# Graph attention over an 8192 x 8192 adjacency: last steps of the row maxima on GpSimd, a sixth PSUM bank in layer 1, x rows on chip, levels by quarters

## The reference

```python
e = leaky_relu(u[:, None] + v[None, :], 0.2)      # 8192 x 8192
e = where(adj > 0, e, -9e15)
att = softmax(e, axis=1)                           # needs the row maximum
h = elu(att @ features)                            # features: 8192 x 64
# layer 0:   x = layernorm(x + elu(att @ ent + x))
# layer 1,2: h = 0.2 * x + 0.8 * elu(att @ (h W)); a small MLP over all h, layernorm
```

## Time and profile before

| what | value |
|---|---|
| median of 3 runs | 3390.24 us (3382.48 to 3395.13) |
| profiled execution | 3391.65 us, its span 3389.8 us |
| mean granted TensorE clock | 0.986 |
| PE / DVE / ACT / POOL busy in the span | 90% / 84% / 67% / 8% |
| DMA moved | 679.11 MB |

### The profile page before, as it was taken

How to read it: one execution, slowest core, us unless ns; L and a number is a source line. 1 busy time by engine, 2 the same in 40 slices (tenths; PEclk the granted TensorE clock), 3 DMA queues, 4 the chain that set the end, 5 groups by cost and what they waited for, 6 DMA issues and landing times. The chain is left out here.

```text
span 3389.8 us, 53702 instructions
## 1 busy us (share of the span) xinstructions
PE 3053.4 (90%) x20369; PEld 1080.6 (32%) x20447; DVE 2862.4 (84%) x5292; ACT 2282.4 (67%) x3934; POOL 287.8 (8%) x330
## 2 busy tenths in 40 slices
PE   1599999999999998799999999997999999999998
PEld 0133333333333333233333333332333333333333
DVE  5688888888888875899999999987888888888886
ACT  0367777777777676577877777774666666666665
POOL 0000000000000000000000000001122112212211
PEclk9999999999999999899999999998999999999999
DMA  9999999999999951312121212216577767766764
GB/s 308 359 347 343 343 343 344 336 346 346 343 343 348 331 157 54 114 64 109 66 106 72 104 75 103 75 63 173 149 163 177 173 158 164 194 161 161 174 142 81
DMA packets 441749, 679.11 MB, mean 200 GB/s; under 512 B 297474, under 2 KB 318082, under 8 KB 416914
## 3 DMA queue, kind: packets, MB, share of 16 engines
q1 hardware_dynamic: 409458, 564.40, 51.3%
q0 software_dynamic: 32032, 111.27, 16.4%
HBM read 430.10 MB, written 77.69 MB: 150 GB/s over the span
## 5 line engine op out<-in xcount | busy, mean ns | idle before, releaser
L1242 DVE SCALAR_TENSOR_TENSOR eps<-ua,v8col,cb 128x512 f32<-128x512 f32 x2800 | 1960.5, 753 | 243.4 <-ACT prob L640 180.1
L640 ACT ACTIVATE prob<-eps,v2col 128x512 f32<-128x512 f32 x2564 | 1641.2, 688 | 635.6 <-PE eps L813 622.6
L854 PE MATMUL acc<-prob,feat 128*64 128x512 f32 x5128 | 1333.7, 599 | 6.3 <-ACT acc_s L645 6.3
L813 PE MATMUL eps<-nt,nbig 128*64 128x512 fp8e4 (+1 forms) x5444 | 1022.5, 386 | 150.6 <-DVE eps L1242 142.8
L813 PEld LDWEIGHTS eps<-nt,nbig 128*64 128x64 bf16 (+1 forms) x5444 | 327.4, 109 | 1115.0 <-DVE eps L1242 726.5
L1051 DVE TENSOR_SCALAR mi<-stage 128x1024 uint8<-128x1024 int32 x512 | 353.5, 692 | 132.7 <-DMA stage<-in_adj_dram 131.5
L854 PEld LDWEIGHTS acc<-prob,feat 128*64 128x64 f32 x5128 | 338.1, 136 | 256.0 <-issue 94.2
L640 ACT ACTIVATE stage<-eps,v2col 128x512 f32<-128x512 f32 x336 | 214.3, 686 | 95.6 <-PE eps L813 93.9
L863 PE MATMUL den<-prob,ones 128*32 128x512 f32 x2048 | 246.4, 599 | 0.0
L1081 DVE TENSOR_SCALAR edges<-nt 128x2048 int32<-128x2048 int32 x192 | 234.1, 1219 | 7.1 <-PE misc L824 7.0
L824 PE MATMUL misc<-edges,oneh 128*32 128x512 fp8e4 x3072 | 190.9, 391 | 52.7 <-DVE edges L1081 37.9
(11 more groups left out here) (174 smaller groups left out, 1686.8 us busy)
## 6 DMA issues: line engine op xcount, KB each, us to landing
stage<-in_adj_dram SPq DMA_DIRECT2D x512, 512.0 KB, 6.4
nt<-nt_d SPq DMA_DIRECT2D x128, 1024.0 KB, 6.1
nt_d<-nt SPq DMA_DIRECT2D x64, 1024.0 KB, 7.1
prob<-prob POOLq DMA_DIRECT2D x96, 512.0 KB, 5.8
stage<-stage POOLq DMA_DIRECT2D x64, 512.0 KB, 6.4
mi<-mi POOLq DMA_DIRECT2D x32, 512.0 KB, 6.5
ub<-u_d SPq DMA_DIRECT2D x48, 256.0 KB, 5.3
xy_d<-xin POOLq DMA_DIRECT2D x32, 256.0 KB, 3.2
```

Source lines behind the costliest of these rows:

```text
L640: nc.scalar.activation(weights(l, b, j), eps[:, j % ES, :], ACT.Exp, bias=v2col[:, j:j + 1]).then_inc(s_p, 1)
L813: mm = nc.tensor.matmul(et[c:c + cols, :], nbig[:, c:c + cols], edge, start=False, stop=True, skip_group_check=True, tile_position=(0, c))
L854: mm = nc.tensor.matmul(acc[h:h + C, :], feat[:, l % 2, j, 0:C], weights(l, b, j), start=(k == 0), stop=(k == NT // 2 - 1))
L1242: dv.scalar_tensor_tensor(eps[:, j % ES, :], ua[:, par, :], v8col[:, j:j + 1], cb[:, par, :], ALU.add, ALU.max).then_inc(s_fill, 1)
```

## The change

1. **GpSimd makes the maxima.** For blocks 1 to 15 of each layer DVE stops at `kmax` (4 operations, now `highest_levels`). The rest is a new `row_maxima` on POOL: one operation ahead of the wait, then 13 in a chain with ten waits on its own results. Block 0 of each layer stays on DVE.
2. **A sixth bank in layer 1.** The idle `den` bank joins the five.
3. **x rows on chip.** Layer 0 reads x from `feat`, where it lies already, and the 16 loads into `xin` go.
4. **Levels by quarters.** `oneh` is made in four parts with a semaphore each, so that PE counts quarter m as soon as it is there. All four edge quarters of the next layer's block 0 are made during the last block before (two were made at the layer's start), two of them in the staging buffer of layer 0.
5. **Steps of edges and counts.** `T_XOR` and `T_HIST` are spread: counts at t = 33, 36, 40, 43 where they stood in pairs at 35 and 43.

The core of the diff:

```diff
+P_STEPS = 10
+HEAD_AT = 5
+BANKS = (ES, ES + 1, ES)
-T_XOR = (29, 32, 40, 41)
-T_HIST = (35, 35, 43, 43)
+T_XOR = (29, 32, 39, 42)
+T_HIST = (33, 36, 40, 43)
...
+        def edge_place(l, b, m):
+            if l > 0 and b == 0 and m >= 2:
+                return spare[:, m - 2, :]
+            return edges[:, m % 2, :]
...
+        def bank(l, j):
+
+            n = j % BANKS[l]
+            return den[:, :] if n == ES else eps[:, n, :]
+
         def freed(l, b, j):
 
-            if j >= ES:
-                return tile(l, b, j) - ES + 1
-            last = max(i for i in range(NT) if i % ES == j)
+            if j >= BANKS[l]:
+                return tile(l, b, j) - BANKS[l] + 1
+            k = l if b else l - 1
+            last = max(i for i in range(NT) if i % BANKS[k] == j % BANKS[k])
             return tile(l, b, last) - NT + 1
...
+            def row_maxima(l, b, par):
+
+                at = P_STEPS * (later(l, b) - 1)
+                u = vucol[:, l % 2, 1, bass.ds(b * RT, RT)]
+                gp = nc.gpsimd
+
+                def step(ins, n):
+                    ins.then_inc(s_pseq, 1)
+                    pool.wait_ge(s_pseq, at + n)
+
+                gp.tensor_scalar(up[:, :], u, ALPHA, None, ALU.mult)
+                pool.wait_ge(s_kmax, later(l, b))
+                gp.tensor_scalar(emp[:, par, :], kmax[:, :], 0.5, None, ALU.is_le)
+                step(gp.tensor_scalar(vm[:, :], kmax[:, :], gst[:, 5:6], gst[:, 7:8], ALU.mult, ALU.add), 1)
+                step(gp.tensor_scalar(vm[:, :], vm[:, :], gst[:, 6:7], None, ALU.max), 2)
+                step(gp.tensor_tensor(ns[:, :], vm[:, :], u, ALU.add), 3)
+                gp.tensor_scalar(r1[:, :], ns[:, :], 0.0, 1.0 - ALPHA, ALU.max, ALU.mult)
+                step(gp.tensor_scalar(nm[:, :], ns[:, :], ALPHA, None, ALU.mult), 4)
+                step(gp.tensor_tensor(nm[:, :], nm[:, :], r1[:, :], ALU.add), 5)
+                step(gp.tensor_tensor(nm[:, :], up[:, :], nm[:, :], ALU.subtract), 6)
+                pool.wait_ge(s_mt, blk(l, b))
+                step(gp.tensor_copy(parts[:, :, 0], nm[:, :]), 7)
+                step(gp.tensor_tensor(r1[:, :], nm[:, :], parts[:, :, 0], ALU.subtract), 8)
+                step(gp.tensor_copy(parts[:, :, 1], r1[:, :]), 9)
+                step(gp.tensor_tensor(nm[:, :], r1[:, :], parts[:, :, 1], ALU.subtract), 10)
+                gp.tensor_copy(parts[:, :, 2], nm[:, :]).then_inc(s_split, 1)
...
             for l in range(2):
                 for b in range(NB):
-                    tail(l, b)
+                    if b > 0:
+                        tail(l, b - 1)
+                    if b < NB - 1:
+                        row_maxima(l, b + 1, 1 - b % 2)
+                tail(l, NB - 1)
             for b in range(NB):
                 for g in range(NT // DEN):
+                    if g == HEAD_AT and b < NB - 1:
+                        row_maxima(2, b + 1, 1 - b % 2)
...
-                pe.wait_ge(s_oneh, l + 1)
                 for m in range(MV):
+                    pe.wait_ge(s_oneh, l * MV + m + 1)
                     count_edges(l, 0, m)
...
-                step(dv.tensor_tensor(oneh[:, :, :], over(kk[:, :], "p (t o) -> p t o"),
-                                      over(iota[:, :], "p (o k) -> p o k"), ALU.is_equal), s_startseq, at + 11)
-                step(dv.tensor_tensor(oneh[:, :, :], oneh[:, :, :], over(ww[:, :].bitcast(F32), "p (t o) -> p t o"),
-                                      ALU.mult), s_startseq, at + 12)
+                for m in range(MV):
+                    q = slice(m * MT, (m + 1) * MT)
+                    dv.tensor_tensor(oneh[:, q, :], over(kk[:, q], "p (t o) -> p t o"),
+                                     over(iota[:, :], "p (o k) -> p o k"), ALU.is_equal).then_inc(s_startseq, 1)
+                    dve.wait_ge(s_startseq, at + 11 + m)
+                    dv.tensor_tensor(oneh[:, q, :], oneh[:, q, :], over(ww[:, q].bitcast(F32), "p (t o) -> p t o"),
+                                     ALU.mult).then_inc(s_oneh, 1)
```

More of the change, by code:

```diff
@@ L301, in blk, with later @@
             return l * NB + b
+        def later(l, b):
+            return l * (NB - 1) + b
         def tile(l, b, j):
@@ L423, in xin_load @@
             def xin_load(l, b):
[L424 to L427, removed]
+                sp.dma_start(xin[:, :, :], xy_v[l - 1, b]).then_inc(s_xin, 16)
             def xin_free(l, b):
-                if b == 0 and l != 1:
+                if b == 0 and l == 2:
                     return
@@ L488, in body @@
                 def body(b, par, head, tail):
-                    if tail:
+                    if tail and l > 0:
                         xin_free(l, b - 1)
@@ L639, in probs @@
                 act.wait_ge(s_z, tile(l, b, j) + 1)
-                nc.scalar.activation(weights(l, b, j), eps[:, j % ES, :], ACT.Exp,
+                nc.scalar.activation(weights(l, b, j), bank(l, j), ACT.Exp,
                                      bias=v2col[:, j:j + 1]).then_inc(s_p, 1)
@@ L803, in mask_scores @@
                 on_act = j in ON_ACT[l]
-                et = eps[:, j % ES, :]
+                et = bank(l, j)
                 m, o = divmod(j, MT)
@@ L824, in count_edges @@
                         mm = nc.tensor.matmul(misc[s * HB:(s + 1) * HB, :], oneh[:, m * MT + j, :],
-                                              half_block(edges[:, n % 2, :], m, j), start=(m == 0 and k == 0),
+                                              half_block(edge_place(l, b, m), m, j), start=(m == 0 and k == 0),
                                               stop=(m == MV - 1 and k == MT // 4 - 1), skip_group_check=True,
@@ L1113, in row_maxima, with highest_levels @@
                      s_headseq, at + 8)
+            def highest_levels(l, b):
+                n = later(l, b) - 1
+                dve.wait_ge(s_fold, blk(l, b) + 1)
+                dve.wait_ge(s_split, blk(l, b))
+                counts = misc[:, 0:RT * HB].bitcast(I32).rearrange("p (r k) -> p r k", k=HB)
+                base = kstep[:, :].rearrange("p (o k) -> p o k", o=1).broadcast_to([P, RT, HB])
+                step(dv.tensor_scalar(he[:, :, :], counts, 23, None, ALU.logical_shift_right), s_kseq, 3 * n + 1)
+                step(dv.scalar_tensor_tensor(hx[:, :, :], he[:, :, :], 0, base, ALU.is_gt, ALU.mult), s_kseq, 3 * n + 2)
+                step(dv.tensor_tensor(hx[:, :, :], hx[:, :, :], he[:, :, :], ALU.add), s_kseq, 3 * n + 3)
+                dv.tensor_reduce(kmax[:, :], hx[:, :, :], AX, ALU.max).then_inc(s_kmax, 1)
             def split_first(l, b, at):
@@ L1156, in tail_elu @@
                 step(dv.tensor_tensor(z[:, :, :], g[:, :, 0:C], spread(rden[:, :]), ALU.mult), seq, at + 3)
-                dve.wait_ge(s_xin, 16 * (blk(l, b) + 1))
                 if l == 0:
-                    step(dv.tensor_tensor(z[:, :, :], z[:, :, :], xin[:, :, 0:C], ALU.add), seq, at + 4)
+                    step(dv.tensor_tensor(z[:, :, :], z[:, :, :], x_rows(b), ALU.add), seq, at + 4)
+                else:
+                    dve.wait_ge(s_xin, 16 * (blk(l, b) - NB + 1))
                 if not (l == 0 and b == 0):
@@ L1343, in _ @@
                     dve.wait_ge(s_oe, 4 * blk(l, 0))
+                    if l == 1:
+                        dv.memset(feat[:, 1, :, C - 1:C], 1.0).then_inc(s_one, 1)
                     bounds(l)
                     levels(l)
-                    for m in range(2, MV):
-                        make_edges(l, 0, m)
                     for part in range(3):
@@ L1365, in body @@
                         if not head_ and l < NLAYER - 1:
-                            for m in range(2):
-                                if t == T_XOR[m + 2]:
+                            for m in range(MV):
+                                if t == T_XOR[m]:
                                     make_edges(l + 1, 0, m)
```

50 lines of the change are left out of this document (35 added, 15 removed).

## The result

| | before | after |
|---|---|---|
| median of 4 runs each, same chip, us | 3389.47 | 3453.02 |
| ratio, 95% interval | | 1.0191, 1.0175 to 1.0208 |
| profiled execution: time, span, us | 3391.65, 3389.8 | 3455.08, 3453.3 |
| mean granted clock | 0.986 | 0.973 |

The change made the kernel slower by 63.6 us. 3370 was predicted, in a range that ends at 3415.

What follows compares the result with a forecast made beforehand. PE was taken to bound layers 0 and 2, PE and DVE level in layer 1. Layer 2 -9, layer 1 -3, layer 0 -1 and between layers -7 us: -20 from 3390.24 gave 3370 us, range 3352 to 3390, span 3305 to 3415.

Steps and rivals of the forecast that it cites:

- which mechanism: POOL's chain after `kmax`: each step waits for the end of a running fill, one per 0.66 us, without holding DVE.
- The rival of a step that is too long for a period: POOL's chain: a step over 0.6 us costs two fills; 3540 us, or 3410 to 3450 if slightly longer; chance 0.16.
- eleven steps; two of them hold two operations that can go through one opening: POOL's chain after `kmax`: 13 operations with ten waits make eleven steps, turn at +7.1 us in layer 1, +6.7 in layer 2.
- The second rival: POOL's chain: each of 13 operations takes its own opening, or DVE is held; gains gone, 3392 us; chance 0.20.
- in the place of waits of about 2 us that go: PE's turn: POOL late by 2.8 us in layer 1 and 1.4 in layer 2, replacing PE's waits for fills.
- a PE that comes 0.8 later, with a sixth bank filled ahead of it, does not wait so: Layer 1 tail: PE's 0.97 us wait for DVE goes, as PE turns 0.8 us later with more filled ahead.
- the forecast's -0.2: Layer 1: turn 0.8 us later, set against the tail wait that goes; -0.2 us a block, -3 us in all.
- the boundaries: Between layers: counting starts 3.7 us sooner with `oneh` in quarters, counts unbroken; twice, -7 us.
- Layer 0: Layer 0: turn unchanged at +6.8 us, 0; the x rows save 16 loads on full DMA engines, -1 us.
- group 5's DMAs: POOL's queue in layer 2: two DMAs behind the chain land at +13.4, taken at +15.5, 2 us to spare: 0.

Runs made afterwards that it cites:

- the filler: Kernel before with only the maxima on GpSimd, plus 14 unused matmuls by PE while it waits at layer 1's turn: 3441.49 us, ratio 1.0160.
- the three kernels compared: Changed kernel (3453.02 us), kernel before with only GpSimd maxima (3460.28 us), and the latter plus 14 unused matmuls in layer 1 (3441.49 us); layer 2 blocks compared by low clock.
- GpSimd alone: Kernel before with only the maxima moved to GpSimd, five banks and the old steps, loads and levels: 3460.28 us, ratio 1.0200.
- The later turn: Changed kernel with the turn at t = 60 instead of 56 and the spread at 61 instead of 57: 3467.46 us, ratio 1.0221.

## Why the prediction was wrong

Of the 84 us between the forecast of -20 and the +63.5 of span, 43 lie in layer 1 and 39 in layer 2.

- **Right: which mechanism.** POOL is paced by the fills, 0.66 us apart; the fills aren't held; ten of them end at +6.6 in layer 1; PE arrives at +4.3; a free step takes 0.27 us (0.25 was taken). The rival of a step that is too long for a period is out: an operation takes 0.20 us alone.
- **Wrong: "eleven steps; two of them hold two operations that can go through one opening".** None of them does: `emp` and `vm`, and likewise `r1` (`r` in the rows) and `nm`, each take an opening of their own. And a scalar read by a pointer takes one more, three of them in the chain. So 16 openings stand where eleven steps were counted. The turn is at +8.35 and +8.00, not at +7.1 and +6.7: 1.25 and 1.3 us too early in the forecast, some 38 us over 30 blocks. The second rival had the first half of this (13 openings, 3392 us); no rival had the pointers.
- **Wrong: a wait of PE was priced by its length.** The forecast put a POOL that is late by 2.8 and 1.4 us "in the place of waits of about 2 us that go", and counted both by their length. The short waits that went (1.4 us in the block of the earlier trace rows) had left the granted clock at 1.00; the one long wait in their place comes with 3.4 us at 0.50. That was in no term: 1.25 us a block in layer 1 by the filler, 1.3 to 2.0 in layer 2 by the blocks compared, 38 to 49 us over 30 blocks.
- **Wrong: "a PE that comes 0.8 later, with a sixth bank filled ahead of it, does not wait so".** The wait in the tail is 0.97 us before and after, with the turn 2.1 us later. So the 0.97 us a block that this was to give back didn't come; the rest of the change gives 0.37. Turn 1.25, clock 1.25 and this 0.97, less 0.37, are the 3.1 us a block between the forecast's -0.2 and the measured +2.89.
- These close the blocks. Layer 1: +2.08 by the turn, +1.25 by the clock, -0.37 by the rest of the change (56.48 against 56.85 us) make +2.96; measured +2.89. That a later turn is a longer block, us for us, was counted on in the forecast and holds both ways: with the head at tile 52 in four parts the turn of layer 1 is 1.14 us sooner than with the old head on DVE and the block 1.15 shorter (1.13 and 1.11 in layer 2). Layer 2: in the three kernels compared, blocks without the stretch of low clock last 66.6 to 66.9 us, 0.5 to 0.8 above before, where the turn is 0.4 to 0.7 later; with it 68.2 to 68.7, and after, where every block has it, 68.21.
- **Right for what the quarters do, not for the sum: the boundaries.** 3.7 us twice were forecast; after, the first is 3.6 shorter and the second 1.2 longer. With the maxima on DVE both are shorter, by 3.5 and 3.1. (By the earlier trace rows three quarters of both operations are 3.4 us, not 3.7.) Timelines of DVE and PE at the first one, in the place of the earlier trace rows:

```profile
1354.10 0.68 DVE L1379 TENSOR_TENSOR oneh<-kk,iota 128x512 bf16<-128x512 int32 x1
...
1355.61 3.61 PE L877 MATMUL misc<-edges,oneh 128*32 128x512 fp8e4 x32 [3.84 <-DVE oneh L1379]
1358.98 2.00 PE L877 MATMUL misc<-stage,oneh 128*32 128x512 fp8e4 x32
```

  The counts start when the first quarter is there and run on without a gap, half of them from the edges in `stage`. The second boundary is 1.2 us longer after. The late turn of the layer's last maxima falls in it: with the maxima back on DVE it is 3.1 us shorter than before, with them on GpSimd and nothing else changed 2.8 us longer.
- **Layer 0 stays open.** -1 us was forecast, -6.2 came, and -9.2 with the maxima on DVE; GpSimd alone has -2.0. x rows on chip or the spread counts may give the rest, but neither was tried alone, and the same code of layer 0 gave -9.2 and -16.7 in two runs.
- **Right by luck: group 5's DMAs** keep their cover. They were to be issued by +7.6, land at +13.4 and be taken at +15.5. They are issued at +8.0 and +8.6, and the second lands at +15.1 to +16.6. PE doesn't wait only because it is itself late, at +17.5 (2894.22 in the block whose `kmax` ends at 2876.70):

```profile
2885.33 1.18 POOL L622 DMA_DIRECT2D mi<-mi  x1
...
2894.22 0.62 PE L930 MATMUL den<-prob,ones 128*32 128x512 f32 x2
```

  The later turn showed the price.
- **Not additive:** the rest of the change saves 0.8% with the maxima on DVE, and 0.1% with them on GpSimd (1.0191 against 1.0200). In layer 2 the low clock comes in every block after, and in 10 of 15 with GpSimd alone. Why it comes in more of them is open.

How much would PE gain with DVE relieved? With one-input fills, where the chain on GpSimd is done in time, the whole change gains 82 us in its one run (ratio 0.976), though with other numbers. With the head left on DVE, one tile later and spread, it gains 55 (0.983). With the maxima on GpSimd beside two-input fills it loses 64.

## What to carry to other kernels

Before a chain of small operations goes to an idle engine, count what each one must wait for there: here each operation on GpSimd that read SBUF, and each scalar by pointer, took one gap between DVE's two-input fills, so a chain that is done at +3.7 beside one-input fills was done at +8.3. Price a wait of PE like those here, of 2.2 us in layer 2 and 4.02 in layer 1, at more than its length, since the granted clock fell with it; the several waits of about half a microsecond that it replaced left the clock alone. And look first at where the small operations stand ahead of the work that the bottleneck waits for: moving the head by one tile and spreading it won 0.9%, where taking it off the engine cost 2.0%.

## What the hardware showed that was not expected

- A GpSimd `tensor_scalar` on 128x4 numbers beside two-input fills: 0.67 us with immediates, 1.25 with one scalar by pointer, 1.96 with two. Beside one-input fills: 0.23, 0.29 and 0.34.
- With PE's wait of 4.02 us in layer 1 the granted clock falls to 0.50 for 3.4 us, from 0.4 us before the wait ends or 1.2 us after it. Fourteen matmuls whose product nobody reads, made in the wait, kept it at 1.00 and made layer 1 17 us shorter.
- The fills aren't slowed by GpSimd here: 3.40 us for five beside the chain and 3.40 for five with hardly any POOL work; five with one input take 3.36.
